# Turning the order of the expert tiles, and storing the sums in one transfer

## What is computed

```python
x = x + tanh(g_xattn) * attention(layernorm(x), ctx, ctx, ...)
x = x + tanh(g_ffn) * ffn(layernorm(x))

def ffn(x):                                   # 2048 tokens, 256 wide
    shared = swiglu(x @ sw1 + sb1) @ sw2 + sb2
    probs = softmax(x @ gate_w + gate_b)      # 8 experts
    topk_probs, topk_idx = top_k(probs, 2)    # each token goes to two experts
    out_e = swiglu(x @ rw1[e] + rb1[e]) @ rw2[e] + rb2[e]
    return shared + sum of out_e over the token's two experts, weighted
```

## Time and profile before

| | |
|---|---|
| median of 3 executions | 699.52 us (698.99 to 710.46) |
| the profiled execution, timed | 703.27 us |
| its span in the profile | 701.4 us |
| PE busy | 627.2 us, 89% of the span |
| DVE, ACT, POOL busy | 482.6, 424.1, 281.0 us |
| from 600 to 680 us: PE busy | 80 of 80 us |
| from 684 us to the end: PE busy | 0 |

### The profile page before, as it was taken

How to read it: one execution, slowest core, us unless ns; L and a number is a source line. 1 busy time by engine, 2 the same in 40 slices (tenths; PEclk the granted TensorE clock), 3 DMA queues, 4 the chain that set the end, 5 groups by cost and what they waited for, 6 DMA issues and landing times.

```text
span 701.4 us, 12642 instructions
## 1 busy us (share of the span) xinstructions
PE 627.2 (89%) x3577; PEld 324.4 (46%) x3577; DVE 482.6 (69%) x804; ACT 424.1 (60%) x842; POOL 281.0 (40%) x318
## 2 busy tenths in 40 slices
PE   4996867999999999999999999999986989999990
PEld 3774632333323323232233333336455768888870
DVE  4788876888887878778688888856675664444430
ACT  4775343777767767677677777786641414555540
POOL 2443242424834654464321113311037532655642
PEclk9999896999999999999999999999998999999995
DMA  8999889565587679569556745005069556665645
GB/s 239 359 263 369 174 266 179 88 106 108 121 218 204 154 153 229 170 116 250 138 83 80 105 66 161 1 13 229 2 219 317 187 196 140 100 104 101 94 46 142
DMA packets 83607, 110.29 MB, mean 157 GB/s; under 512 B 16798, under 2 KB 64841, under 8 KB 82604
## 3 DMA queue, kind: packets, MB, share of 16 engines
q1 hardware_dynamic: 70268, 78.34, 47.3%
q0 software_dynamic: 13296, 31.42, 17.6%
HBM read 64.19 MB, written 47.34 MB: 159 GB/s over the span
## 4 chain that ended last, share of the span: by engine, by line
PE 64%; issue 12%; DMA 8%; POOL 6%; DVE 6%; ACT 1%; POOLq 1%; another core or an unknown queue 0%; SPq 0%; ACTq 0%; DVEq 0%
PE psO L1535 15%; PE psS L1508 15%; PE psM L1490 12%; PE psH L1752 8%; DMA kq<-msb 6%; PE psY L1778 4%; POOL parts L603 3%; PE psH L1709 2%; PE psX L1603 1%; PE psX L1741 1%; PE psH L1763 1%; POOL kq L596 1%; PE psO L1578 1%; PE psM L1508 1%; DMA wA_raw<-wqkv 1%
## 5 line engine op out<-in xcount | busy, mean ns | idle before, releaser
L1142 DVE TENSOR_REDUCE mneg<-psM 128x1 f32<-128x1024 f32 x240 | 282.7, 1219 | 73.8 <-PE psM L1490 73.6
L876 ACT ACTIVATE pr<-psS 128x512 f32<-128x512 f32 x488 | 266.7, 595 | 108.0 <-PE psS L1508 107.9
L1508 PE MATMUL psS<-kq 99*128 99x512 bf16 x488 | 153.0, 387 | 12.7 <-DMA kq<-msb 12.1
L1535 PE MATMUL psO<-pr,vt 128*32 128x512 f32 x1024 | 136.9, 607 | 0.0
L1490 PE MATMUL psM<-kq 96*128 96x512 bf16 x480 | 128.5, 388 | 4.4 <-DVE mneg L1142 2.7
L1508 PEld LDWEIGHTS psS<-kq 99*128 99x128 bf16 x488 | 40.0, 97 | 161.1 <-ACT pr L876 131.3
L585 POOL TENSOR_TENSOR msb<-mcp,none 16x128 bf16<-16x128 f32 x16 | 6.2, 389 | 198.0 <-ACT mcp L853 198.0
L783 POOL DMA_INDIRECT acc<-ysb,ids x39 | 60.2, 1543 | 61.1 <-ACT ysb L999 42.6
L1490 PEld LDWEIGHTS psM<-kq 96*128 96x128 bf16 x480 | 46.7, 98 | 63.6 <-DVE mneg L1142 8.1
L1752 PE MATMUL psH<-wall,zgT 128*128 x234 | 61.0, 396 | 1.4 <-DVE zgT L1373 1.4
L1379 DVE TENSOR_TENSOR rg<-psH,rs 128x256 f32<-128x256 f32 x39 | 16.6, 425 | 57.2 <-ACT rs L987 52.7
(11 more groups left out here) (250 smaller groups left out, 845.2 us busy)
## 6 DMA issues: line engine op xcount, KB each, us to landing
kq<-k_parts SPq DMA_DIRECT2D x96, 128.0 KB, 6.4
wall<-w_parts SPq DMA_DIRECT2D x7, 1536.0 KB
w_parts<-wraw POOLq DMA_DIRECT2D x11, 768.0 KB, 4.9
v_pad<-vst SPq DMA_DIRECT2D x16, 512.0 KB, 8.6
vt<-v_pad SPq DMA_DIRECT2D x16, 512.0 KB, 10.2
k_parts<-parts SPq DMA_DIRECT2D x16, 384.0 KB, 7.1
kq<-q_parts SPq DMA_DIRECT2D x96, 64.0 KB, 6.4
zg<-zs SPq DMA_DIRECT2D x39, 136.0 KB, 2.3
```

The costliest lines, as they stand in the source:

```text
L876: nc.scalar.activation(pr[:, slot, j], score_bank(s, j), ACT.Exp, scale=SCALE).then_inc(e_done, 1)
L1142: V.tensor_reduce(mneg[:, parity, i:i + 1], psM[:, i % 2], X_AXIS, ALU.max, negate=True).then_inc(m_free, 1)
L1508: mm(score_bank(s, j), kst[:, slot, j, kt * P:(kt + 1) * P], qst[:, slot, j], start=True, stop=True).then_inc(s_full, 1)
L1535: last = mm(psO[j * VW:(j + 1) * VW, u % 2], vt[:, u, k, j * VW:(j + 1) * VW], pr[:, k % 4, j], start=(k == 0), stop=(k == KT - 1), skip_g ...
```

## The change

After `r_table` has the tile counts and their running sum, ten new operations on DVE turn the order. For each expert a key of 64 times its tiles plus the end of its run is made; the largest key marks the longest run (of equal ones the last). `shift` is the end of that run, `left` the number of tiles behind it. Then tile i in the order of work is tile `turned[i]` in the order of experts: i + shift, less the total if that has passed it, and i itself for spare tiles. So the experts behind the longest run come first, then those ahead of it, then the longest run, then the spare tiles. The new `gone` is i less the tile's place in its run.

The table's second half (T_E, T_W, T_WAIT) is moved into a function of its own, `r_table_runs`, which DVE calls after `gate(3, 0)`. `tab_ok` now counts to 4: T_ROW has a count of its own, and ACT, TensorE and POOL wait for one more than before. The four stores of the output become one of 2 MB.

```diff
             sp.wait_ge(added, 16 * (TILES_R + 1))
-            for b in range(NB):
-                sp.dma_start(out[b].rearrange("(p r) d -> p (r d)", p=P),
-                             acc[b * NQ:(b + 1) * NQ].rearrange("(p r) d -> p (r d)", p=P)).then_inc(out_st, 16)
-            sp.wait_ge(out_st, 16 * NB)
+            sp.dma_start(out.rearrange("b (p r) d -> (b p) (r d)", p=P // NB),
+                         acc[0:NB * NQ].rearrange("(p r) d -> p (r d)", p=P)).then_inc(out_st, 16)
+            sp.wait_ge(out_st, 16)
...
                 link(V.tensor_tensor(ends, ends, n_t, ALU.add))
+                key, total = tf[:, 0, 3 * NR:4 * NR], ends[:, NR - 1:NR]
+                most, shift, left = (tf[:, 0, 4 * NR + j:4 * NR + j + 1] for j in range(3))
+                link(V.scalar_tensor_tensor(out=key, in0=n_t, scalar=64.0, in1=ends, op0=ALU.mult, op1=ALU.add))
+                link(V.tensor_reduce(most, key, X_AXIS, ALU.max))
+                link(V.scalar_tensor_tensor(out=key, in0=key, scalar=most, in1=ends, op0=ALU.is_ge, op1=ALU.mult))
+                link(V.tensor_reduce(shift, key, X_AXIS, ALU.max))
+                link(V.tensor_tensor(left, total, shift, ALU.subtract))
+                V.tensor_scalar(tf[:, 1], order, left, total, ALU.is_ge, ALU.mult)
+                link(V.tensor_scalar(tf[:, 2], order, total, left, ALU.is_ge, ALU.mult))
+                link(V.scalar_tensor_tensor(out=turned, in0=order, scalar=shift, in1=tf[:, 1], op0=ALU.add, op1=ALU.subtract))
+                link(V.tensor_tensor(turned, turned, tf[:, 2], ALU.add))
...
-                link(V.tensor_tensor(at, order, gone, ALU.subtract))
+                link(V.tensor_tensor(at, turned, gone, ALU.subtract))
+                link(V.tensor_tensor(gone, order, at, ALU.subtract))
                 link(V.tensor_scalar(at, at, float(P), None, ALU.mult))
                 link(V.scalar_tensor_tensor(out=at, in0=e_f, scalar=float(REGION), in1=at, op0=ALU.mult, op1=ALU.add))
-                V.tensor_scalar(tab[:, T_ROW:T_ROW + TAB], at, float(SLOTS - P), None, ALU.min)
+                V.tensor_scalar(tab[:, T_ROW:T_ROW + TAB], at, float(SLOTS - P), None, ALU.min).then_inc(tab_ok, 1)
+
+            def r_table_runs():
+
+                room = cmp[0:1].rearrange("o a r n -> o (a r n)")
+                e_f, gone, at = tf[:, 1], tf[:, 2], tf[:, 3]
+                dve.wait_ge(tab_ok, 2)
                 link(V.tensor_copy(tab[:, T_E:T_E + TAB], e_f))
...
             gate(3, 0)
+            r_table_runs()
             base(1)
```

11 lines of the change are left out of this document (6 added, 5 removed).

## The result

| | before | changed |
|---|---|---|
| device time, median of 20 runs each, same chip | 701.26 us (695.76 to 713.99) | 707.71 us (700.87 to 719.36) |
| ratio of the runs, with its 95% interval | 1 | 1.0077 [1.0045, 1.0109] |
| the profiled execution: time, span | 703.3, 701.4 | 711.8, 709.9 |

Against 2% the two are the same. (A ratio leaves out executions more than 1.5% above the fastest of their kernel, the changed kernel's profiled one among them, and so need not be the quotient of the medians; what follows compares stretches, not spans.)

What follows compares the result with a forecast made beforehand. POOL's adds were taken to end the kernel, with DVE's way to `base(1)` on the path before the tiles. +1.3 (DVE) - 2.3 (turn) - 0.8 (store) = -1.8 us gave 697.7 us; whole range 694.5 to 701.5.

Steps and rivals of the forecast that it cites:

- The chain of adds: POOL's 39 adds end the kernel; with the order turned, seven named adds wait and the last starts 2.3 us earlier.
- flights: On POOL, a wait's whole price from one add's start to that of the next run's first: 5.0 us.
- The rival of long flights: POOL's five close waits cost more, likely 5.7 us each, so the turn stops paying; time 701.2, chance 0.13.
- the one by which the change doesn't do what it says: Rival: another landing ends the chain of adds, so the turn gains nothing; time 700.0, chance 0.07.
- the 5.5 that the prediction names as a sign of being wrong: Waits of 5.5 us or more between runs of tiles on POOL would show the forecast wrong.
- about 3 us instead of 5.8: Sign of being right: how long after the last result POOL's last add starts.
- The store: At the end, one 2 MB store for four gains 0.8 us, range -1.6 to +1.6.
- The work on DVE: Table operations ahead of `base(1)` delay it and every tile by 1.3 us, range 0.9 to 2.1.
- the hole is the memset's: DVE's 1.14 us idle before `base(1)` was put down to POOL's memset, fixed in time, so new work partly fills it.
- The delay of 1.9: Delay of `base(1)` if the idle time before it is not the memset's; it would make the sum 0.6 us higher.
- TensorE's clock falls: Rival: idling before `second(2)` drops the clock to 1.2 GHz, costing 1.5 us; sum +0.3, time 699.8, chance 0.10.
- the one from the span to the time: The timed median was taken as 1.9 us below the profiled span, turning 699.6 into 697.7.

Runs made afterwards that it cites:

- e4_old_order: Changed kernel with only the turn undone (the last new operation copies the old order), added work and one store kept; 717.7 us beside 713.1, ratio 1.0094.
- e6: Kernel before with POOL's memset of the bias rows moved in front of its last eight scatters; 719.4 us beside 711.0, ratio 1.0109.
- e7: Changed kernel with DVE's table work later and POOL's memset in front of the last scatters; 713.0 us beside 711.0, ratio 1.0001.
- n_after: Changed kernel with no edit, timed again on chip 3; median 716.3 us over 6 runs beside 717.0, no interval.
- e8_table_mid: Changed kernel timed again with no edit, whatever its label says; 715.8 us beside 711.0, ratio 1.0077.
- n2_before: Kernel before, unchanged, timed as if it were another kernel on chip 4; 707.5 us beside 699.2, ratio 1.0090.
- e1: Kernel before with ten one-element DVE memsets behind the tile loop, which nothing waits for; 714.3 us beside 713.1, ratio 0.9957.
- e9: Changed kernel with the row table in front of `base(1)` and the table's other half behind `gated_low(3, 1)`; 710.7 us beside 717.0, ratio 0.9894.
- n_before: Kernel before, unchanged, timed as if it were another kernel on chip 3; 718.3 us beside 717.0, ratio 1.0038.

## Why the prediction was right or wrong

**The chain of adds held.** The waiting adds were 3, 10, 18, 20, 21, 24 and 26. The five flights behind the long queue had a mean of (4.69 + 5.71 + 4.64 + 4.73 + 5.13) / 5 = 4.98 us, 5.0 was used, and the stretch from first to last add went from 101.8 to 99.4 in the mean of six profiles: -2.4 for a predicted -2.3. e4_old_order shows that it is the turn. The rival of long flights is out, and so is the one by which the change doesn't do what it says. One wait, in front of add 20, was 5.7 to 5.9 us in all six profiles, over the 5.5 that the prediction names as a sign of being wrong; but the sum goes by the mean. The last add began 697.37 - 694.57 = 2.8 us behind the end of the last result. The prediction has "about 3 us instead of 5.8"; its 5.8 is counted from the start of that operation, and from its end it was 688.13 - 682.84 = 5.3.

**The store** gained 0.7 us alone and 0.4 in the mean of the changed kernel's six profiles, for a predicted 0.8. The prediction's estimate from the Trainium skill ("DMA: Bandwidth & Descriptors", section "Anatomy of one DMA — SWDGE (gpsimd) path"), 6.8 us for the one transfer, does not fit: it took 8.3 us to land.

**The work on DVE was dearer than its term.** `base(1)` came 13.93 to 14.16 us behind the counts, against 12.3 to 12.5 in the profiles of the old sequence but one: +1.6, where the sum has 1.3 and the range goes to 2.1. `base(0)` took +0.9 of it, not 0.6: two comparisons that read a scalar from memory lasted 0.29 us each, and the next one 0.25. And the six moved operations took 578.76 - 576.79 = 1.97 us instead of 1.30, because the first of them, the cast, took 1.09 us beside POOL's memset, where the earlier trace rows has 0.42. 0.9 + 2.0, less the hole of 1.1 to 1.3 that is now filled, is 1.6 to 1.8. The step "the hole is the memset's" was wrong: the Trainium skill ("SBUF — State Buffer", section "Who interferes with whom") says that a DVE instruction with one input in SBUF, outside the two-port modes, does not contend with GpSimd, and e6 and e7 agree, since the hole stayed where it was with the memset long over. The delay of 1.9 that was worked out from it was too much by 0.3, since the hole was filled all the same.

**The step of the sum that failed is the clock's.** The sum has nothing for TensorE's clock. The rival "TensorE's clock falls" had 0.10, with the argument that the clock stood at 1.00 in the window before `second(2)` in spite of the idling. In five of six profiles of the changed kernel it fell to 1.2 GHz, in four of them behind the wait for `base(1)`, and so it did in e4. The price was right: the first add comes 33.2 to 33.4 us behind the counts where the clock fell and 31.71 in n_after where it did not, 1.6 for a forecast of 1.5.

What was wrong is the length of the idling. The prediction added 1.3 to 2 us to the 0.33 of its one profile, which gives 1.6 to 2.3. But in that profile `first(3, 1)` had pauses and ended just before `second(2)`; that this changes from execution to execution one profile could not show. In n_after it had pauses too, and the idling was 1.70 us, as forecast, and the clock held, as forecast. In the four it had few pauses or none, the idling was 2.86 to 4.29 us, and the clock fell. (The fifth, e8_table_mid, fell inside `first(3, 1)`, as two of the seven profiles with the old work on DVE did.)

So the stretch from the counts on comes to +1.6 for `base(1)`, +1.3 for the clock (1.6 in five of six, one of which is not the change's), -2.4 and -0.4: +0.1 us, near the +0.3 of that rival. The profiles say the same: from the counts to the end 145.14 us in the mean of six (144.02 to 145.83), against 145.15 and 145.17 before; with n2_before, the one without the hole, the kernel before has 144.7 in the mean, and the change +0.4. With e1 and e6, which have the old work, order and stores as well, the mean of five is 145.18, and the change 0.0. The forecast -1.8 would have needed the clock to stay. Where it did, in n_after, the stretch took 144.02, 1.1 less than before; the other 0.7 are mainly the 0.3 more at `base(1)` and a store of 9.20, which gained 0.2 instead of 0.8.

**What put the time outside the range is another step, the one from the span to the time.** The clock's 1.3 us account for little of the 10 us between the predicted 697.7 and the measured 707.7. The prediction took 1.9 us off the profiled span, by the median of three runs (699.0 to 710.5), and let the time move from there only by what the change does. It had nothing for how far the level of one kernel moves from series to series, and the runs show 8 us and more. The same kernel has medians of 699.2, 701.3, 711.0, 713.1 and 717.0 us from one series and chip to another, and 699.2 and 707.5 in two series on one chip. The changed kernel's 707.7 lies among those of the unchanged one. Of the measured +0.8% there remains no part that the experiments tie to the change. The prediction called 2% about what a measurement can tell, and yet gave a range of 1%. What stays open is why the attention stage's loads land in 6.4 us in one execution and in 7.3 in another, why the first series had the two kernels 6.5 us apart on one chip, and why TensorE pauses inside `first(3, 1)` in some executions and not in others.

## What to carry to other kernels

Before a difference of under 1% is explained, the unchanged kernel has to be timed in the changed one's place; here it gave 1.009 against itself. What an edit does is then read from the first instruction that is the same in both, not from the span: ahead of it the six profiles of the changed kernel scatter by 13.6 us, behind it by 1.8. And work that is added in front of the one instruction for which TensorE waits can cost twice, once as delay and once as TensorE's clock (in five of the seven profiles with this work, e4 among them). So it goes into a hole or behind that instruction, and how long TensorE will idle has to be read from more than one profile.

## What the runs showed of the hardware

**A cast and a memset.** DVE's cast of 40 numbers took 1.09 us beside POOL's memset of 1.08 us, and ended with it; clear of the memset, 0.17 us (n2_before). In the kernel before it took 0.42 us, and ended with POOL's issue of a scatter:

```profile
562.13 0.98 POOL L741 DMA_INDIRECT zs<-zx,slot_u  x1 [0.31 <-issue]
```

In e9 it was a `TENSOR_SCALAR` of the same size; DVE's and POOL's rows:

```profile
566.54 0.99 DVE L1310 TENSOR_SCALAR tf<-tf 1x40 f32<-1x40 f32 x1
```

```profile
566.40 1.08 POOL L772 MEMSET brow<- 128x1152 f32 x1
```

In all three POOL's instruction had begun first. The section "Who interferes with whom" of the Trainium skill's page "SBUF — State Buffer" has the rule: a copy, a cast or a `tensor_scalar` may run in a mode that takes the port pair shared with GpSimd, and then the one that was issued second waits for the other. The three rows agree; that these instructions ran in that mode no row shows. Nor is it the whole of a scatter's issue that holds them: in n2_before the cast ran in its 0.17 us although such an issue had begun 0.13 us ahead of it.

**And the other way round.** POOL's issue of a scatter takes 0.98 us. The one in front of the memset took 1.31 us in before and n_before, and 2.17 in the changed kernel's first profile (1.54 to 2.17 in the six), beginning 0.04 us before DVE's two `gated_low`, each with two inputs in SBUF; in n2_before, where POOL's scatters stand otherwise, it is another one, again beside `gated_low`, 2.19:

```profile
561.87 0.99 POOL L741 DMA_INDIRECT zs<-zx,slot_u  x1 [0.30 <-issue]
563.16 2.19 POOL L741 DMA_INDIRECT zs<-zx,slot_u  x1 [0.30 <-issue]
565.65 0.98 POOL L741 DMA_INDIRECT zs<-zx,slot_u  x1 [0.30 <-issue]
```

The section of the Trainium skill named above states that a DVE instruction with two inputs in SBUF contends with a GpSimd instruction that reads SBUF. The stretched issues fit that; that the issue of a scatter is such an instruction no row shows. On POOL itself the longer issue cost nothing, but it moved the memset from 11.1 to 12.0 us behind the counts, and there the cast met it.

**A transfer of 2 MB from memory to memory** landed in 8.3 us, and the span ended 8.6 to 9.2 us behind its issue. With four of 512 KB, issued in 2.54 us, it was 9.2 to 9.5. The mean gain was 0.7 us in the kernel before and 0.4 in the changed one; what part of it is the issuing and what part the longer rows no run tells apart.

**TensorE's clock.** In 18 profiles the granted clock fell to 1.2 GHz behind the six longest idle times in front of `second(2)`, 2.83 to 4.29 us, and at `second(2)` behind none of 2.48 us or less. In three more it fell inside a group of products with pauses of 0.25 to 0.92 us. Each fall made the first add 1.5 to 1.7 us later.
